# Cross attention, units of 512 queries: value products in pairs, maxima spread over twelve blocks by a table of banks, denominators closed one unit later

## What is computed

```python
q = _split_heads(Q @ Wq_w.T + Wq_b)          # Q = layernorm(x), 4 x 1024 x 512, 16 heads of 32
k = _split_heads(K @ Wk_w.T + Wk_b)          # K = V = context, 4 x 1601 x 512
v = _split_heads(V @ Wv_w.T + Wv_b)
scores = jnp.einsum('bhqd,bhkd->bhqk', q, k) / np.sqrt(DK)
scores = jnp.where(mask == 0, -1000000000.0, scores)
attn = jax.nn.softmax(scores, axis=-1)
out = jnp.einsum('bhqk,bhkd->bhqd', attn, v)
```

## Time and profile before

| | |
|---|---|
| median of 3 runs | 3818.74 us |
| profiled execution: time, span | 3817.16 us, 3815.3 us |
| TensorE matmul busy | 3730.7 us, 98% of the span |
| VectorE busy | 2386.6 us, 63% |
| GpSimd busy | 1687.6 us, 44% |
| ScalarE busy | 1434.0 us, 38% |
| mean granted TensorE clock | 0.993 |
| cross attention, 32 units | from 1232 to 2958 us of the span |

### The profile page before, as it was taken

One profiled execution on the slowest core, in us unless ns is written; L12 is line 12 of the kernel. 1 busy time (PEld: TensorE's weight loads), 2 busy tenths in 40 slices (PEclk: granted clock), 3 DMA queues, 4 the chain that ended last, 5 costly groups with the idle time before them and its releaser, 6 DMA issues. The chain is left out here.

```text
span 3815.3 us, 62978 instructions
## 1 busy us (share of the span) xinstructions
PE 3730.7 (98%) x18664; PEld 2480.3 (65%) x18665; DVE 2386.6 (63%) x6129; ACT 1434.0 (38%) x1793; POOL 1687.6 (44%) x984
## 2 busy tenths in 40 slices
PE   8999999999988999999999999999999999999998
PEld 7888888788876544444444444454444777777886
DVE  6544444344466888888888888888888543434235
ACT  3222222222333455545555455545555221222332
POOL 2222222200023776677666766676665222312334
PEclk9999999999999999999999999999999999999999
DMA  6444444555565122222211222222211434327679
GB/s 203 125 128 131 134 121 121 162 199 187 180 196 180 36 58 58 58 56 58 58 29 34 58 58 59 58 56 58 48 31 40 157 123 138 111 89 257 213 279 340
DMA packets 245485, 446.75 MB, mean 117 GB/s; under 512 B 20024, under 2 KB 104536, under 8 KB 241244
## 3 DMA queue, kind: packets, MB, share of 16 engines
q1 hardware_dynamic: 215196, 366.37, 33.3%
q0 software_dynamic: 14752, 49.29, 3.6%
q10 hardware_dynamic: 15264, 27.79, 1.9%
HBM read 262.21 MB, written 181.17 MB: 116 GB/s over the span
## 5 line engine op out<-in xcount | busy, mean ns | idle before, releaser
L1165 DVE CUSTOM_DVE_ANT_0 xf_unread<-xa_mx_ps,mask_q 128x402 bf16<-128x402 f32 x1984 | 1033.7, 574 | 279.0 <-PE xa_mx_ps L1158 152.8
L1788 ACT ACTIVATE probs<-xa_scores 128x1024 f32<-128x1024 f32 (+1 forms) x416 | 417.5, 1024 | 417.6 <-PE xa_scores L1662 411.5
L1788 ACT ACTIVATE xa_probs<-xa_scores 128x1024 f32<-128x1024 f32 (+1 forms) x416 | 417.3, 1024 | 387.0 <-PE xa_scores L1662 387.0
L1662 PE MATMUL xa_scores<-mask_t,ident_b 128*128 128x512 bf16 (+1 forms) x1664 | 549.4, 388 | 0.0
L1623 POOL TENSOR_TENSOR xa_sums<-xa_sums,xa_probs 128x1024 f32<-128x1024 f32 x220 | 519.6, 2383 | 18.1 <-POOL xa_sums L1623 15.9
L1623 POOL TENSOR_TENSOR xa_sums<-xa_sums,probs 128x1024 f32<-128x1024 f32 x220 | 519.4, 2380 | 18.1 <-POOL xa_sums L1623 14.6
L1158 PE MATMUL xa_mx_ps<-xa_kp,queries 96*128 96x402 f32 x1024 | 364.7, 418 | 0.0
L1158 PE MATMUL xa_mx_ps<-xf_kp,queries 96*128 96x402 f32 x960 | 342.1, 418 | 0.0
L1656 PE MATMUL xa_scores<-queries,xf_kp 97*128 97x512 f32 (+1 forms) x832 | 284.7, 423 | 15.1 <-ACTq L1810 8.3
L1158 PEld LDWEIGHTS xa_mx_ps<-xa_kp,queries 96*128 96x128 f32 x1024 | 181.7, 189 | 169.4 <-DVE xf_maxima L1165 107.8
L1656 PE MATMUL xa_scores<-queries,xa_kp 97*128 97x512 f32 (+1 forms) x832 | 284.5, 423 | 1.8 <-ACT probs L1788 1.8
(11 more groups left out here) (418 smaller groups left out, 7258.4 us busy)
## 6 DMA issues: line engine op xcount, KB each, us to landing
turned_p<-rows SPq DMA_DIRECT2D x31, 1024.0 KB, 3.8
rows<-turned_p SPq DMA_DIRECT2D x124, 256.0 KB, 4.6
bridge_rows<-sorted_in SPq DMA_DIRECT2D x78, 256.0 KB, 3.3
sorted_out<-ex_made ACTq DMA_DIRECT2D x78, 256.0 KB, 4.3
queries<-qT_high SPq DMA_DIRECT2D x30, 512.0 KB
xf_kp<-kT_high SPq DMA_DIRECT2D x16, 800.5 KB, 11.8
xa_kp<-kT_high SPq DMA_DIRECT2D x16, 800.5 KB
rows<-in_ctx SPq DMA_DIRECT2D x16, 768.0 KB, 4.8
```

The source lines that it names most:

```text
L1165: return dve.tensor_tensor_reduce(out=unread[slot % 2][:, :], in0=scores[:, 0:MKEYS], in1=mask_q[:, half * QB + qt, MFIRST[kb]:MFIRST[kb] ...
L1662: last = pe.matmul(scores[pr][0:keys, jj, :], ident_b[0:keys, 0:keys], mask_t[0:keys, kt, queries], start=False, stop=True)
L1788: act.activation(prob[ring][pr][0:keys, :, :], scores[pr][0:keys, :, :], ACT.Exp, scale=SCALE).then_inc(exped, 1)
```

## The change

Five edits, all in `cross_attention`:

- **Weighing in pairs.** `WEIGHED_AT`: rounds 1, 3, 5, 7, 9 and 11 weigh two blocks each, one behind the other, rounds 0, 2, 4, 6, 8 and 10 none; block 12 alone in round 12.
- **Twelve blocks of maxima.** `SLOTS_AT`: rounds 10, 11 and 12 of unit u take the first 3, 3 and 2 slots of unit u + 2, then rounds 0 to 8 of the next unit the rest: 2, 8, 6, 8, 5, 8, 6, 8, 5. Beside the second pair's masks a round now has two places for a slot where it had one. `BANKS` says which bank a slot uses: the sums' bank 1 is left out from slot 4 to slot 11, from slot 12 on the banks go round in threes as before.
- **Sums closed one unit later.** `add_up(u - 1)` runs in round 0 of unit u, ScalarE's `keep_sum(u - 1)` behind the exponentials of that round.
- **Reciprocal of 16 columns.** All 32 partitions of a head hold the same sum. `invert` turns `sum_sb` in squares of 32, takes the reciprocal of one column per square (128 x 16) and turns it back with each column read 32 times. Its four instructions, the product last, stand before the reads of slots 14, 16, 17 and 18 (`INVERSION` counts from slot 10, the first of round 1).
- The vector engine's additions of blocks 9, 10 and 11 stand between the reads of the early slots: 3 reads, block 9, 3 reads, block 10, 2 reads, block 11. The tensor engine and ScalarE use the loop form with the first unit outside.

```diff
@@ -1465,10 +1465,23 @@
-    SLOTS_OF = [2, 7, 8, 8, 8, 8, 8, 8, 7] + [0] * (KT - 9)
-    SLOT_OF = [sum(SLOTS_OF[:n]) for n in range(KT + 1)]
-    assert SLOT_OF[KT] == SLOTS
+    SLOTS_AT = {10: 3, 11: 3, 12: 2, 0: 2, 1: 8, 2: 6, 3: 8, 4: 5, 5: 8, 6: 6, 7: 8, 8: 5}
+    EARLY = (10, 11, 12)
+    SLOTS_OF, first_slot = {}, 0
+    for kt, count in SLOTS_AT.items():
+        SLOTS_OF[kt] = range(first_slot, first_slot + count)
+        first_slot += count
+    assert first_slot == SLOTS
+    AHEAD = SLOTS_OF[EARLY[-1]].stop
+    BANKS = [1, 2, 0, 1, 2, 0, 2, 0, 2, 0]
+    BANKS += [(2, 0, 1)[n % 3] for n in range(SLOTS - len(BANKS))]
+    SUM_BANK = 1
+    BEFORE_SUMS = max(n for n in range(AHEAD) if BANKS[n] == SUM_BANK)
+    AFTER_SUMS = min(n for n in range(AHEAD, SLOTS) if BANKS[n] == SUM_BANK)
+    AFTER_PEAKS = BANKS.index(0)
     TURN = 9
+    WEIGHED_AT = {1: (0, 1), 3: (2, 3), 5: (4, 5), 7: (6, 7), 9: (8, 9), 11: (10, 11), 12: (12,)}
+    INVERSION = {4: 0, 6: 1, 7: 2, 8: 3}
     OWN = {"pool": tuple(range(9)), "dve": (9, 10, 11)}
@@ -1638,8 +1652,9 @@
             def _(pe):
                 def mx(u, par, half, slot):
                     m = SLOTS * u + slot
-                    pe.wait_ge(mx_read, m + 2)
-                    scores_of_slot(pe, mx_ps[slot % 3], qp[par], kp[par], half, slot).then_inc(mx_made, 1)
+                    back = next(n for n in range(1, SLOTS) if BANKS[slot - n] == BANKS[slot])
+                    pe.wait_ge(mx_read, m - back + 5)
+                    scores_of_slot(pe, mx_ps[BANKS[slot]], qp[par], kp[par], half, slot).then_inc(mx_made, 1)
...
                         pe.wait_ge(sum_kept, u + 2)
+                        if ahead:
+                            pe.wait_ge(mx_read, SLOTS * (u + 2) + BEFORE_SUMS + 5)
@@ -1713,38 +1730,49 @@
                     for kt in range(KT):
-                        slots = iter(range(SLOT_OF[kt], SLOT_OF[kt + 1]) if more else ())
+                        early = kt in EARLY
+                        slots = iter(SLOTS_OF.get(kt, ()) if (ahead if early else more) else ())
+                        if first and kt == 0:
+                            slots = iter(range(AHEAD + len(SLOTS_OF[0])))
 
                         def maxima(most):
                             for slot in itertools.islice(slots, most):
-                                mx(u + 1, *nxt, slot)
-
+                                if early and slot == AFTER_PEAKS:
+                                    pe.wait_ge(row_kept, u + 4)
+                                if slot == AFTER_SUMS:
+                                    pe.wait_ge(sum_kept, u + 2)
+                                if early:
+                                    mx(u + 2, 1 - par, half, slot)
+                                else:
+                                    mx(u + 1, *nxt, slot)
+
+                        if ahead and kt == EARLY[0] and half == 0:
+                            pe.wait_ge(loaded, 16 * (LOADS * (u // HALF + 1)))
                         following = (u, par, half, kt + 1) if kt + 1 < KT else (u + 1, *nxt, 0) if more else None
-                        between = 1 if kt else 0
                         for pr in range(PAIRS) if following else ():
                             score(*following, pr)
                             if pr == 1:
-                                maxima(between)
+                                maxima(1)
                             add_mask(following[2], following[3], pr, 0)
-                            if pr == 0:
-                                maxima(between)
+                            maxima(1)
                             add_mask(following[2], following[3], pr, 1)
                             if pr == 0:
-                                maxima(between)
+                                maxima(1)
                         if more and kt == TURN:
                             turn_peaks(u + 1)
-                        maxima(2 * between)
-                        weigh(u, par, kt, (at + kt) % RING)
-                        if more and kt == 0:
-                            pe.wait_ge(row_kept, u + 3)
-                            pe.wait_ge(sum_kept, u + 2)
-                            if half == 1:
-                                pe.wait_ge(loaded, 16 * (LOADS * (u // HALF + 1)))
-                        maxima(SLOTS_OF[kt])
+                        maxima(2)
+                        if kt == 0 and not first:
+                            add_up(u - 1, OWN)
+                        for due in WEIGHED_AT.get(kt, ()):
+                            weigh(u, par, due, (at + due) % RING, ahead)
+                        maxima(SLOTS)
                         if not more and kt < DC:
                             turn_output_weight(kt)
-                    add_up(u, OWN if more else OWN_LAST)
+                    if not more:
+                        add_up(u, OWN_LAST)
@@ -1788,12 +1816,18 @@
 
+                def keep_sum(u, half):
+                    act.wait_ge(total_made, u + 3)
+                    act.activation(sum_sb[half][:, :], sum_ps[:, :], ACT.Copy).then_inc(sum_kept, 1)
...
                             exp(u + 1, 0, (at + KT) % RING, OWN)
+                        if kt == 0 and not (isinstance(u, int) and u == 0):
@@ -1839,13 +1873,27 @@
 
+                def invert(u, half, part):
+                    mine = sum_sb[half]
+                    if part == 0:
+                        dve.wait_ge(sum_kept, u + 3)
+                        dve.transpose(mine[:, :], mine[:, :]).then_inc(inverted, 1)
+                    elif part == 1:
+                        dve.wait_ge(inverted, 3 * u + 1 + 3)
+                        dve.reciprocal(inverse[:, :], mine[:, 0:BANK:DK]).then_inc(inverted, 1)
+                    elif part == 2:
+                        dve.wait_ge(inverted, 3 * u + 2 + 3)
+                        dve.transpose(mine[:, :].rearrange("p (c d) -> p c d", d=DK),
+                                      inverse[:, :].unsqueeze(2).broadcast_to([P, BANK // DK, DK])).then_inc(inverted, 1)
+                    else:
+                        dve.wait_ge(inverted, 3 * u + 3 + 3)
+                        dve.wait_ge(o_kept, u + 3)
+                        dve.wait_ge(stored, 16 * (u + 2))
+                        dve.tensor_tensor(out[:, :], o_sb[half][:, :], mine[:, :], ALU.mult).then_inc(finished, 1)
@@ -1876,16 +1924,18 @@
-                    for slot in range(SLOTS) if more else ():
+                    first = isinstance(u, int) and u == 0
+                    ahead = not (isinstance(u, int) and u == units - 2)
+                    for slot in range(0 if first else AHEAD, SLOTS):
+                        if slot - SLOTS_OF[1].start in INVERSION and not first:
+                            invert(u - 1, 1 - half, INVERSION[slot - SLOTS_OF[1].start])
                         read(u + 1, 1 - half, slot)
-                    if more:
-                        peak(u + 1)
-                        for i, kt in enumerate(OWN["dve"]):
-                            for pr in range(PAIRS):
-                                add(u, kt, (at + kt) % RING, i, pr, POOL_ADDS)
-                    if not (isinstance(u, int) and u == 0):
-                        finish(u - 1, 1 - half)
+                    peak(u + 1)
+                    for i, kt in enumerate(OWN["dve"]):
+                        for slot in SLOTS_OF[EARLY[i]] if ahead else ():
+                            read(u + 2, half, slot)
+                        for pr in range(PAIRS):
+                            add(u, kt, (at + kt) % RING, i, pr, POOL_ADDS)
```

More of the change, by code:

```diff
@@ L1805, in unit @@
                     act.activation(o_sb[half][:, :], o_ps[:, :], ACT.Copy).then_inc(o_kept, 1)
-                    act.wait_ge(total_made, u + 3)
-                    act.activation(sum_sb[half][:, :], sum_ps[:, :], ACT.Copy).then_inc(sum_kept, 1)
+                    if not more:
+                        keep_sum(u, half)
                 act.sem_inc(row_kept, 3)
```

24 lines of the change are left out of this document (12 added, 12 removed).

## The result

The changed kernel takes **3874.15 us** (median of four executions, 3867.19 to 3878.32), the kernel before 3820.17 beside it: a ratio of 1.014 [1.0128, 1.0153]. I had said slower, 3835, and a range up to 3858. The direction was right, the size was not: it lost 54 us where I had 16.

What follows compares the result with a forecast made beforehand. TensorE was taken as the bound, held up a little by the reads. Per unit -1.6 - 0.6 + 1.5 + 1.5 + 0.1 = +0.9 us, taken as +0.7; 20 us over 29 units less 1.5 gave 3835 us, range 3790 to 3858.

Steps and rivals of the forecast that it cites:

- An ordinary unit: Middle units: 54.3 us, +0.7 us each after a little taken off the summed +0.9, 20 us over 29 units.
- Inversion: Four pieces among the reads of slots 14 to 18: slots 20 to 23 wait for banks, 1.5 us more a unit.
- Distance of the slots: Closer slots: the sixth waits 0.25 us for its bank in six rounds, 1.5 us a unit; old waits of 0.6 go.
- Pairs: Entries and exits of the weighing fall from 13 to 8 a unit at 0.32 us each: 1.6 us saved.
- Sums one unit later: `add_up` in round 0: GpSimd starts at 3.4 instead of 2.3 us; the last addition is in time by half a microsecond.
- the sum ring: GpSimd, additions, reads and `add_up` as a closed ring: 50.3 us, shorter than the unit; rival that it binds, 3850, chance 0.08.
- 4.31 - 7 x 0.19 - 0.87: Seven-slot round less its slots and weighing: 2.15 us remain for scores, masks and entering and leaving the weighing.
- the product 0.69: Inversion's last piece, between the reads of slots 16 to 18: priced at 0.69 us, 0.8 with a read's accumulator first.
- the edge units: Unit 30 loses eight slots, 1.5 us less; units 0 and 31 come out even.
- a place with nothing to wait for: Where `add_up` stood before its move to 2.3 us into round 0; no cost was given for leaving it.
- rival of mine: Inversion and spacing hidden, 3770 or 3799 (0.22 for all faster); no change, 3811 to 3826 (0.20); sum ring binds, 3850 (0.08).
- even: Unit 0 gets eight slots but has no inversion; unit 31 has rounds of two exponentials' length instead of weighings': no net cost.

Runs made afterwards that it cites:

- e1_gaps: Changed kernel with the inversion's four pieces behind the pairs of weighings of rounds 1, 3, 5 and 7; 1.0037 of the kernel before.
- e3_end: Changed kernel with the whole inversion and product behind the unit's last addition, where GpSimd is idle; 1.0039 of the kernel before.
- e8_five_end: Changed kernel with the inversion at the unit's end and five maxima ahead of a weighing instead of six; 1.001 of the kernel before.
- e7_single_end: Changed kernel with every block weighed in its own round and the inversion behind the unit's last addition; 1.0133 of the kernel before.
- e2_single: Changed kernel with every block weighed in its own round instead of in pairs; 1.0526 of the kernel before.
- e6_single_small_pool: Changed kernel with single weighings and GpSimd's additions behind the first block cut to 16 of 512 columns, sums incomplete; 1.0201 of the kernel before.
- e15_cover: Changed kernel with the eight matmuls that weigh block 12 issued twice in every unit, output not the reference's; 3911 us in one execution.
- e4_flat_pe: Changed kernel with TensorE's 32 units written out instead of looped, other engines keeping their loops; 1.0074 of the kernel before.
- e5_stagger: Changed kernel with TensorE's loop shifted by one unit against the other engines', two units written out ahead of it; 1.0208 of the kernel before.
- e9_three_last: Changed kernel with inversion at the unit's end, five maxima ahead of a weighing, and blocks 10 to 12 weighed together; 1.0034 of the kernel before.

## Why the prediction was wrong

Point by point, forecast and measured:

- *The whole*: the profiled execution lost 50.0 us of span where I had 19. Of the 31 between them 12.4 are the jumps and 11.4 units 28 to 30; an ordinary unit's 0.13 us above forecast makes 3.5.
- *An ordinary unit*: 54.3 forecast, 54.36 to 54.58 measured, so +0.83 us over before where I had +0.7; 22 us over 27 units. This is the part of the loss that I had priced, and it came. Odd rounds 5.6, measured 5.64; round 2 4.6, 4.27; round 6 3.2, 3.20 to 3.25; rounds 4 and 8 2.8, 2.76 to 2.80; round 9 3.9, 4.17; round 10 2.5, 2.49; round 12 4.3, 4.27; round 0 3.5, 3.41.
- *Inversion*: the pieces cost 0.71, 0.25, 0.71 and 0.69 as said where nothing held them, their place 1.04 us in round 2 (e1_gaps) and 0.9 over the unit against an inversion at its end (e3_end), instead of 1.5.
- *Distance of the slots*: a quarter microsecond in rounds 3, 5 and 7, shown by e8_five_end (5.64 to 5.40). e7_single_end, which has the new slots but neither pairs nor the inversion among the reads, is 1.2 us a unit above before, where I had 0.9 and 0.1.
- *Pairs*: 1.2 us a unit against single weighings, where I had 1.6.
- So the ordinary unit came out near its forecast in part by luck: I had the inversion's place 0.6 us too dear, the gain of the pairs 0.4 too high and the slots 0.2 too cheap.
- *Sums one unit later*: no wait of `add_up` was seen in ordinary units; the sum ring didn't bind. GpSimd began at 3.70 us, not 3.4.
- *Arithmetic*: 4.31 - 7 x 0.19 - 0.87 is 2.11, not 2.15, and 3836 with the median's 1.6 on top is 3838, not 3835. Neither changes a reading.

**The step that failed** is the step *Inversion* where it says "the product 0.69", as a price that holds wherever the product is put, and with it the words on the edge units, which give unit 30 1.5 us less and name no cost for 28 and 29. A second term was put at nothing without a reason: the moved `add_up`, below. The 0.69 was read where GpSimd was idle: its last additions end at 1817.45, the product stands at 1828.38. The change moved it under GpSimd's additions. In units 1 to 27 it escaped by 0.04 to 0.08 us, in units 28 to 30 it did not: 11.4 us, and 3.2% where every unit is hit, as e2_single against e6_single_small_pool shows. The Trainium skill has this rule ("SBUF — State Buffer", Who interferes with whom): a VectorE instruction with two SBUF inputs and a GpSimd instruction that reads SBUF exclude each other, and the one issued first keeps the other out for its whole length; a VectorE instruction with one SBUF input at most, outside the two-port modes, stays out of this. The traces agree in both directions, 2.74 us for the product that came second and 2.87 instead of 2.38 for the addition that did, and so do the transpositions with their one input, 0.70 to 0.71 us in all units. Which of two was issued first the records don't tell when they start within some 0.04 us of each other: such a product is free in units 1 to 27 here and held in three units of e15_cover. No rival of mine named it.

The second gap, of the same size, is the jump. I moved `add_up` behind it at no cost ("a place with nothing to wait for") and didn't ask what its eight matmuls covered: 12.4 us with the clock's share (e4_flat_pe takes the jumps away, e15_cover puts cover back). The Trainium skill ("Runtime: NRT & Kernel Launch", Instruction fetch mechanics) says that a taken branch out of the instruction window waits for a fetch; TensorE's branch records, 3.3 to 4.9 us when taken and 0.08 when not, agree with it, though no run here shows a fetch.

The last 7 us (a start 3.3 later, units 0 and 31) are not explained beyond that units 0 and 31 have other rounds ("even" in the forecast for both was wrong by 1.6 and 2.1); the later start lies ahead of the changed stage, and kernels that are the same up to there start it between 1235.25 and 1242.06, so it is likely spread and not the change.

## What to carry to other kernels

A price read from a row holds for the neighbours that the row had: before moving an instruction, look at what the other engines do at the new place, GpSimd above all when it reads two tiles of SBUF. Work that looks idle-free and movable can be the cover of something else; look for the loop's jump on every engine and for what is queued ahead of it. When one stall is taken away and nothing is gained, look for the next engine's stall of the same kind.

## What the runs showed that I had not expected

A taken loop branch keeps TensorE's stream 3.3 to 4.9 us and VectorE's 2.8 to 3.2. ScalarE's it keeps 2.7 to 3.3 us in the kernel before and 0.23 in the changed one, GpSimd's 0.28 and the sync engine's 0.18; what makes the difference is open. Behind a jump the length of TensorE's stand went with the clock: in all runs with its loop but e5_stagger, 36 of 44 stands of 1.7 to 2.4 us were followed by a stretch at 1.2 GHz, and 2 of 16 of 0.9 to 1.6 us (the two: 0.89 in e9_three_last and 1.58 in e15_cover). And a product of 0.69 us, held in every unit, cost the kernel 3.2%.
